# A two-layer graph network over an 8192-node graph on one core: TensorE sums the slots of the step in front before it packs the next tile of adjacency

## The reference

```python
# layer 0: attention over each node's neighbours
h = relu(layernorm(x)); H = h @ W.T + b
s, r = H @ a_s, H @ a_r
e = leaky_relu(A * s + A * r.T, 0.2)
x = x + softmax(where(A > 0, e, -9e15), axis=1) @ H
# layer 1: sum over neighbours, then maximum over neighbours
h = relu(layernorm(x)) @ weight
out = relu(A @ h + bias)
x = x + (for each row of A: maximum of out over its nonzero columns)
```

## Time and profile before

| what | us |
|---|---|
| median of 3 runs | 2659.04 |
| lowest and highest of them | 2654.21, 2662.23 |
| the profiled execution, its own time | 2658.55 |
| its span on the core | 2656.8 |
| PE busy | 1292.3 |
| DVE busy | 1519.5 |
| POOL busy | 1422.1 |
| ACT busy | 465.0 |

### The profile page before, as it was taken

How to read it: one execution, slowest core, us unless ns; L and a number is a source line. 1 busy time by engine, 2 the same in 40 slices (tenths; PEclk the granted TensorE clock), 3 DMA queues, 4 the chain that set the end, 5 groups by cost and what they waited for, 6 DMA issues and landing times.

```text
span 2656.8 us, 20293 instructions
## 1 busy us (share of the span) xinstructions
PE 1292.3 (49%) x5093; PEld 670.8 (25%) x5093; DVE 1519.5 (57%) x3498; ACT 465.0 (18%) x1561; POOL 1422.1 (54%) x1465
## 2 busy tenths in 40 slices
PE   3765145636153645533445997862442212475036
PEld 1432023313032312323441443320111100132013
DVE  6888757866442625436244654454658755893234
ACT  1541134502122402443450000000000000000000
POOL 0002655461746463567535556366757775567763
PEclk8887668777676866765676998885676555687568
DMA  9999857787773879852343223114112321212221
GB/s 343 398 372 410 266 164 281 283 278 295 265 288 107 329 249 380 343 180 66 81 132 81 71 63 80 30 48 89 51 45 67 91 75 36 53 50 52 71 69 44
DMA packets 161767, 443.50 MB, mean 167 GB/s; under 512 B 31986, under 2 KB 90661, under 8 KB 128750
## 3 DMA queue, kind: packets, MB, share of 16 engines
q1 hardware_dynamic: 78974, 307.90, 30.4%
q0 software_dynamic: 49360, 108.63, 15.9%
q10 hardware_dynamic: 33312, 25.63, 3.2%
HBM read 404.00 MB, written 37.98 MB: 166 GB/s over the span
## 4 chain that ended last, share of the span: by engine, by line
DVE 20%; PE 17%; another core or an unknown queue 17%; issue 16%; DVEq 11%; POOL 10%; SPq 3%; DMA 3%; ACT 2%; ACTq 0%; POOLq 0%
PE psV L1210 10%; POOL ring L758 6%; POOL rec_all L758 4%; DVE words L1375 2%; DVEq L1374 2%; PE psV L1037 2%; DMA a_buf<-in_adj 2%; DVE words L1366 2%; DVE words L1370 2%; DVEq L1369 2%; PE psH L1093 2%; SPq L479 2%; PE psV L1231 1%; DVEq L1486 1%
## 5 line engine op out<-in xcount | busy, mean ns | idle before, releaser
L684 POOL DMA_INDIRECT ring<-h_table,srec x505 | 496.1, 982 | 292.6 <-issue 150.0
L1037 PE MATMUL psV<-a_buf,bit_ident 128*128 128x512 bf16 x1024 | 326.7, 486 | 219.7 <-DMA a_buf<-in_adj 148.2
L758 POOL DMA_INDIRECT rec_all<-p_table,srec x325 | 320.6, 986 | 190.7 <-issue 97.8
L1231 PE MATMUL psV<-a_buf,trec 128*128 128x512 f32 (+1 forms) x398 | 237.3, 751 | 256.3 <-DVEq L1717 102.6
L1093 PE MATMUL psH<-ring,ident 128*128 128x128 f32 x1010 | 159.3, 320 | 149.5 <-remote 60.6
L1037 PEld LDWEIGHTS psV<-a_buf,bit_ident 128*128 128x128 bf16 x1024 | 117.5, 117 | 410.9 <-issue 305.2
L1210 PE MATMUL psV<-rec_all,a_buf 128*128 128x512 bf16 x888 | 205.6, 388 | 26.8 <-issue 26.2
L717 POOL DMA_INDIRECT ring<-y_table,srec x191 | 185.0, 968 | 60.8 <-issue 60.2
L1231 PEld LDWEIGHTS psV<-a_buf,trec 128*128 128x128 f32 x398 | 95.5, 248 | 394.7 <-issue 186.6
L1093 PEld LDWEIGHTS psH<-ring,ident 128*128 128x128 f32 x1010 | 152.3, 234 | 160.5 <-issue 146.9
L1231 PE MATMUL psH<-a_buf,trec 128*128 128x512 f32 x124 | 79.6, 776 | 211.3 <-DVEq L1486 139.5
(11 more groups left out here) (259 smaller groups left out, 2299.6 us busy)
## 6 DMA issues: line engine op xcount, KB each, us to landing
a_buf<-in_adj SPq DMA_DIRECT2D x256, 1024.0 KB
ring<-h_table,srec POOLq DMA_INDIRECT x505
trec<-records ACTq DMA_DIRECT2D x63, 128.0 KB
packed<-wbuf ACTq DMA_DIRECT2D x28, 256.0 KB
a_buf<-packed SPq DMA_DIRECT2D x7, 1024.0 KB
rec_all<-p_table,srec POOLq DMA_INDIRECT x325
h_table<-stage POOLq DMA_DIRECT2D x16, 258.0 KB, 8.1
a_buf<-r_row SPq DMA_DIRECT2D x1, 4096.0 KB
```

The source lines that it names most:

```text
L684: pool.indirect_dma_start(ring[:, A_AT[q] + j, :], None, h_table, bass.IndirectOffsetOnAxis(srec_u[g][:, i, LIST + j:LIST + j + 1], 0)).th ...
L758: pool.indirect_dma_start(ring[:, at + j, 0:D] if at < RING else side[:, at - RING + j, :], None, p_table, bass.IndirectOffsetOnAxis(slot, ...
L1037: last = pe.matmul(psV[n % 2][:, h * BANK:(h + 1) * BANK].rearrange("p (g n) -> p g n", n=P), bit_ident[:, k, :], rows[:, :, k, :], start= ...
L1231: pe.matmul(psO[b % len(psO)][:, 0:width], results[:, n % RESULTS, :], hot[:, c % HOT, at:at + width], start=(ranked_tile(n) == FIRST[g]), ...
```

## The change

In each turn of TensorE's loop the loop over `sum_slots` moves from behind pack and numbering to in front of them. No instruction is added, dropped or altered, and the order on the other four engines is the same as before.

```diff
             for n in range(LAST + 1):
+                for q in AT_STEP[n - 1]:
+                    sum_slots(q)
                 if n + 1 < T:
                     pack(n + 1)
                 if n + 1 < T - 1:
                     number_words(n + 1)
-                for q in AT_STEP[n - 1]:
-                    sum_slots(q)
                 if n in TURNS:
                     turn_rows(n)
```

## The result

The changed kernel takes 2721.81 us (median of 4 runs, 2721.26 to 2727.5), the kernel before 2656.62 (4 runs, 2649.83 to 2662.23): ratio 1.0257, 95 % interval 1.0233 to 1.028. It is 65 us slower; the prediction said 11 us slower and ended its range at 2694. The sign held, the size did not.

A forecast was written before the change was run, and what follows sets the result against it. No engine passes 57 % busy, so waits between engines were taken to set the end. 5.7 + 2.3 - 4.2 + 1.2 + 3.0 + 3.3 = 11.3 us on 2658.55 gave 2669.9, stated as 2670 us, range 2646 to 2694.

The forecast's parts named there:

- Term 1: Steps 19 to 26: the pack, now behind the sum, delays word copy, numbering and VectorE's extractions; +5.7 us.
- the ring: Steps 19 to 26: ScalarE and TensorE alternate through scaling, sum, pack, word copy, normalising, raw scores; six turns, 112.4 us.
- D(27): Start of VectorE's list extraction of step 27; 4 to 8 us late was the sign to look for.
- The clock, weighed: Packs that follow a sum were priced at 3.8 us; at the lower clock 21 us more, 2691 not 2670.
- Term 2: Steps 27 to 53, tiles with many slots: most delays taken as absorbed in slow stretches; +2.3 us.
- The class counting: Step 46, third group: it follows the later pack, and ranking, record scatters and next gathers hang on it; +2.3 us.
- the three extractions: VectorE's list extractions of steps 36, 40 and 42: 3.7 us late each, counted as 0, 11 as the other bound.
- Term 3: Steps 54 to 62, small sums: -4.2, +1.2, +3.0 and +3.3 us at steps 56, 58, 61 and 62.
- The -4.2 us of step 56: Step 56: sums of q=29 and q=30 run while pack(57) is held, not between it and the turning of rows.
- A: Rival, faster: a large sum such as that of q=20 slips out of a slow stretch; 2650; chance 0.15.
- B: Rival, no change: VectorE's slack takes Term 1 and steps 58 to 62 are covered; 2658 to 2664; chance 0.27.
- C: Rival, nothing absorbed: extractions of steps 36 to 49 and part of the clock's 21 us; +30 to +45, 2695; chance 0.13.

The follow-up runs named there:

- x1_after: The changed kernel as it is, on a chip without slow stretches: 2306.57 us, ratio 1.0109 (1.0092 to 1.0126) against the kernel before.
- x6_dense: The kernel before with the sums in front of the pack in steps 19 to 26 only, on a chip without slow stretches: ratio 1.0042 (1.0029 to 1.0055).
- e1_dense: The kernel before with the sums in front of the pack in steps 19 to 26 only: 2686.88 us, ratio 1.0064 (1.0031 to 1.0096).
- e2_mid: The kernel before with the sums in front of the pack in steps 27 to 53 only: 2720.43 us, ratio 1.019 (1.0125 to 1.0256).
- e11_scatter: The kernel before with the sums in front of the pack in steps 46 to 48 only, chip without slow stretches: 2293.56 us, ratio 1.0053.
- e9_two: The kernel before with the sums in front of the pack in steps 27 and 28 only: 2681.41 us, ratio 1.0054 (1.0025 to 1.0083).
- e3_late: The kernel before with the sums in front of the pack in steps 54 to 62 only: 2670.21 us, ratio 1.0028 (1.0001 to 1.0055).
- e4_held: The kernel before with the sums in front of the pack in steps 54, 55 and 56 only: 2661.57 us, ratio 0.9987 (0.9961 to 1.0013).
- e6: The kernel before with GpSimd waiting for landing after each six gathers of a tile: 2681.56 us, ratio 1.0068 (1.0035 to 1.0102).
- The window: The kernel before with at most ten gathers under way from q=16 on, run only on chips without slow stretches: ratio 1.000 (0.9991 to 1.001).
- x2_before: The kernel before, unchanged, traced on a chip without slow stretches: ratio 0.9997 (0.9987 to 1.0007).

## Why the prediction failed, step by step

**Term 1, steps 19 to 26.** The mechanism was right. The turn of the ring with q=4 was put at 18.2 us; in x1_after the exponentials of q=4 and q=5 begin 18.7 us apart (380.49 and 399.15), and the six turns take 115.4 us in place of 112.4. The term was 5.7 us. Measured without stretches are 9 us (x6_dense) and 17 with them (e1_dense), and D(27) is 10.2 and 23.6 us late where 4 to 8 were named as the sign. The first mis-sized number is the sum at 0.22 us a slot, a price that no row shown has: the earlier trace rows had nine slots in 4.18 us after idling, 0.24 us a slot. It now stands first behind the wait and runs at the lower clock:

```profile
400.51 5.03 PE L1093 MATMUL psH<-ring,ident 128*128 128x128 f32 x22 [5.44 <-ACT trec L853]
...
405.77 2.81 PE L1093 MATMUL psH<-ring,ident 128*128 128x128 f32 x20
```

These are q=2 and q=3 in the changed kernel, 0.46 us a slot at a granted clock of 0.50, the lower level, and then 0.28 at 0.85; the pack behind them takes 3.78 us at 1.00. **The clock, weighed** looked for the price at the packs, which indeed come at 3.78, and missed it at the sums. The Trainium skill (TensorE: Matmul & The Clock Gate, What's actually happening), cited there, says that activity releases the higher rate. By that rule the first work behind a wait pays, whichever it is, and these rows agree. The second number is the caught word copy of pack(23) shown above, 8.4 us, and one of 6.3 us at pack(25), neither of which has a counterpart before or on the chips without stretches.

**Term 2, steps 27 to 53**, held the error: +2.3 us forecast, 51 measured (33 to 68, e2_mid). The class counting, those +2.3 us, was about right: in x1_after the scatters of the third group begin 12.0 us late, where GpSimd was 10.2 us late just ahead of them, so 1.8. The step that failed is the one that put everything else at nothing because a slow stretch would cover it, "absorbed there: 0" for the three extractions and "which covers that: 0, with 13 as the bound" for the load of tile 39. The extractions alone came out nearly so, with a lag of 40.4 us at step 32 and 41.3 at step 44 in the changed kernel, though e2_mid goes from 21.6 to 29.5. What was left out is what happens to a pack that has lost its lead. Before, a pack had ended long before VectorE needed it. Behind the sum it is late itself, so are the loads that it releases, and at steps 46 to 48 this is 12 us on a chip without stretches (e11_scatter). On a chip with them the middle steps cost 51 us, because engines are held there that were not held before: a small shift against GpSimd's series goes with the loss of a whole extraction, at steps 30 to 32 through two small sums (e9_two, 14 us), and the handovers of steps 47 to 50 are caught in the record scatters and the gathers behind them. The prediction had the rows of such stretches and read them only as cover, in which a delay vanishes, never as a trap, in which what has not begun can wait for the end.

**Term 3, steps 54 to 62**, was +3.3 us. Measured are 7 us with an interval of 0 to 15 (e3_late), and 1 to 2 us in x1_after, where VectorE's lag goes from 22.0 at step 53 to 22.8 at 62 and the spans end 24.2 apart. The -4.2 us of step 56 is there, 56.2 to 52.1 us of lag from step 56 to 57 in the changed kernel, but it is given back, 56.9 at step 62; e4_held, that step and its neighbours alone, is 0.9987 (0.9961 to 1.0013), which 4 us would fit as well as none.

**The rivals.** A's sign appeared and its gain did not: the 32 matmuls of q=20 took 4.9 us in the changed kernel and not 19.5, under the 8 that were named, but they began at 885.1 and not at 834.3, since ScalarE had been held ahead of them, for 43.6 us (834.5 to 878.1) where it had been 31.5 before. B had the covered steps. C named the right direction, "nothing is absorbed", with +30 to +45 us, and by its kind of reason (packs and clock) it would still have been short by 20: the price is not the pack but what a shifted engine meets. The last sentence of the prediction, that the slow stretches "hold more time than all my terms", was the one to act on.

**What stays open.** What a stretch is made of. An engine is held in it behind a late handover (ScalarE at pack(23)) and without one (VectorE at extraction 31), and which of its instructions are let through is not known (extraction 39 of the kernel before was). Pauses for landing remove it at q=16 (e6), which fits a backlog of gathers as well as it fits GpSimd's lack of a gap. The window would tell these apart, and no run has it on a chip with stretches. Why one chip shows them and another not, no run tells. No kernel tried is faster than the kernel before on its chip.

## What to carry to other kernels

An engine's lead over its consumer is a resource like a buffer. Before putting work with a wait ahead of work without one, write down for each later step how long the second had been finished before it was used, what loads it releases, and whether the new time of the handover falls where handovers are slow. A slow stretch in a trace is cover for some delays and a trap for others, and which of the two has to be measured. And price the first matmuls behind a wait at the lower clock, whichever they are.

## What the hardware showed

The same kernel took 2657 to 2669 us in three sets of runs and 2282 on two other chips, with equal work (VectorE 1519.5 and 1523.3 us busy, GpSimd 1422.1 and 1421.7). The page of x2_before:

```profile
PE 1243.8 (55%) x5093; PEld 650.4 (29%) x5093; DVE 1523.3 (67%) x3498; ACT 465.0 (20%) x1561; POOL 1421.7 (62%) x1465
```

On the former the receivers of TensorE's work stand still for 148 us in the window above, on the latter 5; 172 us of the difference have gathered by step 62, the rest comes behind the stream. A change that costs 1.1 % on one chip costs 2.6 % on another, so a comparison of two kernels needs both on one chip, and a trace of each sort tells more than repeated times.
